# Twelve-row small products, values first, 128x128 filter tiles, shared filter copies and POOL in the block inversion

## What is computed

```
q = silu(dwconv(hs @ Wq, conv_q))        # causal convolutions with 4 taps over the tokens
k = silu(dwconv(hs @ Wk, conv_k))
v = silu(dwconv(hs @ Wv, conv_v))
beta = sigmoid(hs @ Wb)                  # one per head, 4 heads
q, k = l2norm(q), l2norm(k)              # per head: needs sums of squares over 64 channels
attn = where(strict, -(kb @ k.T), 0)     # in chunks of 32 tokens, kb = k * beta
T = inv(eye(32) - attn)                  # one unit triangular 32x32 inverse per chunk and head
fir = dwconv(v, 3 taps), dwconv(v, 15 taps), dwconv(v, 64 taps)   # per channel
```

## Time and profile before

| | |
|---|---|
| runs of the kernel | 1622.45, 1614.07, 1622.11 us; median 1622.11 |
| profiled execution | 1622.37 us, its span 1620.6 us |
| mean granted PE clock | 0.888 of full speed |
| PE busy | 1453.7 us (90%) |
| DVE, ACT, POOL busy | 878.0 (54%), 673.9 (42%), 527.5 (33%) us |
| the block in question | about 13 to 371 us of the span |

### The profile page before, as it was taken

How to read it: one execution, slowest core, us unless ns; L and a number is a source line. 1 busy time by engine, 2 the same in 40 slices (tenths; PEclk the granted TensorE clock), 3 DMA queues, 4 the chain that set the end, 5 groups by cost and what they waited for, 6 DMA issues and landing times. The chain is left out here.

```text
span 1620.6 us, 25691 instructions
## 1 busy us (share of the span) xinstructions
PE 1453.7 (90%) x8444; PEld 1138.4 (70%) x8445; DVE 878.0 (54%) x1708; ACT 673.9 (42%) x1269; POOL 527.5 (33%) x460
## 2 busy tenths in 40 slices
PE   4999976996999999939999999997979999999995
PEld 1666676985888888728888888884656666666643
DVE  4576636964999999934443444435622212212186
ACT  3333325995777777722333333331112222222214
POOL 3445510001455555523221222110314444444311
PEclk9778755557999999959999999977989999999998
DMA  3795365544333333213222201114011111111164
GB/s 86 158 223 151 102 193 146 139 154 118 98 92 91 91 95 92 59 54 107 69 95 95 77 30 60 43 40 146 14 52 55 56 57 55 57 57 55 49 201 136
DMA packets 149371, 151.89 MB, mean 94 GB/s; under 512 B 63952, under 2 KB 115760, under 8 KB 147760
## 3 DMA queue, kind: packets, MB, share of 16 engines
q1 hardware_dynamic: 136368, 117.34, 24.7%
q0 software_dynamic: 8320, 29.37, 7.0%
q10 hardware_dynamic: 4608, 4.20, 0.7%
HBM read 98.43 MB, written 42.99 MB: 87 GB/s over the span
## 5 line engine op out<-in xcount | busy, mean ns | idle before, releaser
L2405 DVE TENSOR_TENSOR hidden<-unit_psum,gate 128x352 f32<-128x352 f32 x72 | 37.8, 525 | 210.2 <-ACT gate L2368 210.2
L1818 POOL TENSOR_TENSOR scores<-scores,score_max 128x1024 f32<-128x1024 f32 x32 | 60.7, 1896 | 247.9 <-DVE score_max L1746 247.9
L498 PE MATMUL proj_psum<-window,toep 96*96 96x128 f32 x512 | 116.7, 401 | 22.0 <-DMA toep<-in_fir 11.5
L498 PEld LDWEIGHTS proj_psum<-window,toep 96*96 96x96 f32 x512 | 111.6, 256 | 26.9 <-DMA toep<-in_fir 15.6
L431 PE MATMUL proj_psum<-filtered 128*128 128x512 f32 x192 | 106.1, 705 | 24.4 <-DMA filtered<-in_xT 22.0
L569 ACT ACTIVATE filtered<-proj_psum 32x512 f32 (+1 forms) x192 | 112.7, 587 | 36.6 <-PE proj_psum L498 32.1
L618 DVE SCALAR_TENSOR_TENSOR filtered<-proj_psum,conv_taps,filtered 128x508 f32<-128x508 f32 (+1 forms) x144 | 95.5, 734 | 56.3 <-ACT filtered L523 56.3
L2336 PE MATMUL unit_psum<-wd,hiddenT 128*128 (+1 forms) x432 | 111.9, 395 | 13.7 <-issue 12.6
L2267 POOL DMA_INDIRECT unit_rows<-x_rows,token_of_slot x72 | 69.9, 970 | 127.1 <-PE unit_psum L2310 104.6
L2274 POOL DMA_INDIRECT outs<-unit_out,choice_of_slot x72 | 71.1, 987 | 99.3 <-DVE unit_out L2410 96.7
L2336 PEld LDWEIGHTS unit_psum<-wd,hiddenT 128*128 128x128 f32 (+1 forms) x432 | 76.4, 190 | 36.5 <-issue 28.8
(11 more groups left out here) (283 smaller groups left out, 3305.6 us busy)
## 6 DMA issues: line engine op xcount, KB each, us to landing
neg_decay_blocks<-in_gw1s POOLq DMA_DIRECT2D x8, 1280.0 KB, 9.7
ndg<-filtered SPq DMA_DIRECT2D x8, 1024.0 KB, 4.6
neg_decay_gram<-ndg SPq DMA_DIRECT2D x16, 512.0 KB, 3.8
ctxT_tiles<-in_ctxT SPq DMA_DIRECT2D x16, 512.0 KB, 3.6
gathered<-outs SPq DMA_DIRECT2D x32, 256.0 KB, 3.0
toep<-in_fir SPq DMA_DIRECT2D x64, 96.0 KB, 2.1
window<-value SPq DMA_DIRECT2D x32, 192.0 KB, 2.9
filtered<-in_xT SPq DMA_DIRECT2D x8, 512.0 KB, 4.3
```

Of the source, the lines that this page charges most:

```text
L498: mm = pe.matmul(fir_psum[0:NFIR * QUART, u, TC * w + c, :], toep[:, w, :, :, c].rearrange("p f t -> p (f t)"), window[:, u, :, :, TC * w ...
L1818: pool.tensor_tensor(sc[:, i % 2, t, :, :], sc[:, i % 2, t, :, :], wide(mx[:, t, :], [128, XH, L], 2), ALU.subtract).then_inc(shifted[t], 1)
```

## The change

- **Small products.** `small_rows` puts a 12-column selector (`small_weights`, 128 x 12) in the array and streams 512 columns of squares past it, 4 products, and 2 more with `Wb` over x. The result is 12 rows by 512 tokens. ACT copies it to SBUF (`keep_rows`), and `small_turn` turns it with four transposes. The copy of `Wb` into the selector is made by DVE before PE starts.
- **Order.** Values are projected first (2, 0, 1), the products of `small` come one block later around `projections(1)`, and each engine's order is rewritten to go with it. SP issues the chunk 2 windows and the rest of the tiles ahead of its waits for the last block's stores. The loops over chunks are written out.
- **Filters.** `toep` is laid out by channel, 128 x 128 for each, the rows from 96 and the columns from 96 being zero, and `window` has 128 rows. A half's transfer is one instead of two, with 4 KB a row of 96 rows.
- **Copies.** In chunks 0 to 4 and 15, DVE takes 4 of 12 pieces (even chunks) or 8 of 12 (odd ones).
- **Inversion.** POOL makes the product of group 1; DVE keeps the product of group 0 and both sums. DVE comes to the inversion after its copies of chunks 0 to 4.

```diff
+            def small_rows(n):
+                u = n % 2
+                pe.wait_ge(squared[0], n + 1)
+                pe.wait_ge(squared[1], n + 1)
+
+                pe.wait_ge(tanh_done, n)
+                pe.wait_ge(ssq_kept, n)
+                for t in range(2 * KD):
+                    pe.matmul(psum[0:3 * H, S_BANK, :], small_w[:, t, :], squares[:, u, t, :], start=(t == 0), stop=False)
+                for k in range(KD):
+                    mm = pe.matmul(psum[0:3 * H, S_BANK, :], small_w[:, 2 * KD + k, :], xT[:, u, k, :], start=False, stop=(k == KD - 1))
+                mm.then_inc(rows_mm, 1)
+
+            def small_turn(n):
+                pe.wait_ge(rows_kept, n + 1)
                 for q in range(BB):
-                    tok = slice(q * L, q * L + L)
-                    for t in range(2 * KD):
-                        pe.matmul(psum[:, S_BANK, 12 * q + 2 * t:12 * q + 2 * t + 2], squares[:, u, t, tok],
-                                  headsel[:, :], start=True, stop=True)
-                    for k in range(KD):
-                        mm = pe.matmul(psum[:, S_BANK, 12 * q + 8:12 * q + 12], xT[:, u, k, tok], wb[:, k, :],
-                                       start=(k == 0), stop=(k == KD - 1))
+                    mm = pe.transpose(psum[:, S_BANK, 3 * H * q:3 * H * q + 3 * H], small[0:3 * H, q * L:q * L + L],
+                                      M.ident[0:3 * H, 0:3 * H])
...
-                        mm = pe.matmul(fir_psum[0:NFIR * QUART, u, TC * w + c, :], toep[:, w, :, :, c].rearrange("p f t -> p (f t)"),
+                        mm = pe.matmul(fir_psum[:, u, TC * w + c, :], toep[:, w, c, :],
                                        window[:, u, :, :, TC * w + c].rearrange("p q b -> p (q b)"), start=True, stop=True)
                     mm.then_inc(half_done[w], 1)
 
+            for n in range(NBLK):
+                projections(2)(n)
+                if n >= 1:
+                    turn_values(1)(n - 1)
+                projections(0)(n)
+                if n >= 2:
+                    grams(0)(n - 2)
+                if n >= 1:
+                    small_rows(n - 1)
+                projections(1)(n)
+                if n >= 1:
+                    small_turn(n - 1)
+                if n >= 2:
+                    grams(1)(n - 2)
+                turn_values(0)(n)
+            last = NBLK - 1
+            turn_values(1)(last)
+            grams(0)(last - 1)
+            grams(1)(last - 1)
+            small_rows(last)
+            small_turn(last)
...
+        SHARED_CHUNKS = {0, 1, 2, 3, 4, NFC - 1}
+
+        def pieces(n, by_dve):
+
+            first = (2 - n % 2) if n in SHARED_CHUNKS else NFIR
+            return [(q, f) for f in (range(first, NFIR) if by_dve else range(first)) for q in range(NQ)]
...
+            for n in range(NBLK):
+                if n >= 2:
+                    decays(n - 2)
+                convolutions(2)(n)
+                if n >= 2:
+                    scale_grams(0)(n - 2)
+                convolutions(0)(n)
+                if n >= 1:
+                    keep_squares(n - 1)
+                if n >= 2:
+                    scale_grams(1)(n - 2)
+                convolutions(1)(n)
+            last = NBLK - 1
+            decays(last - 1)
+            scale_grams(0)(last - 1)
+            scale_grams(1)(last - 1)
+            keep_squares(last)
+            keep_pieces(0)
+            decays(last)
+            scale_grams(0)(last)
+            scale_grams(1)(last)
+            for n in range(1, 5):
+                keep_pieces(n)
 
             dve.wait_ge(nd_in, 32)
-
             for i in range(1, CB):
-                for g in range(2):
-                    blocks = slice(2 * g, 2 * g + 2)
-
-                    if i > 1:
-                        dve.wait_ge(inv_row[g], i - 1)
-                    p = prod[:, g, :, 0:i * i].rearrange("p c (k j) -> p c k j", j=i)
-                    dve.tensor_tensor(p, inv[:, blocks, 0:i, 0:i], wide(nd[:, blocks, i, 0:i], [128, 2, i, i], 2),
-                                      ALU.mult).then_inc(inv_mul[g], 1)
+                if i > 1:
+                    dve.wait_ge(inv_row[0], i - 1)
+                p = prod[:, 0, :, 0:i * i].rearrange("p c (k j) -> p c k j", j=i)
+                dve.tensor_tensor(p, inv[:, 0:2, 0:i, 0:i], wide(nd[:, 0:2, i, 0:i], [128, 2, i, i], 2),
+                                  ALU.mult).then_inc(inv_mul[0], 1)
                 for g in range(2):
                     blocks = slice(2 * g, 2 * g + 2)
                     dve.wait_ge(inv_mul[g], i)
                     p = prod[:, g, :, 0:i * i].rearrange("p c (k j) -> p c k j", j=i)
                     dve.tensor_reduce(inv[:, blocks, 0:i, i], p, AX.X, ALU.add).then_inc(inv_row[g], 1)
+
+            for n in range(5, NFC):
+                keep_pieces(n)
...
+            for i in range(1, CB):
+                if i > 1:
+                    pool.wait_ge(inv_row[1], i - 1)
+                p = prod[:, 1, :, 0:i * i].rearrange("p c (k j) -> p c k j", j=i)
+                pool.tensor_tensor(p, inv[:, 2:4, 0:i, 0:i], wide(nd[:, 2:4, i, 0:i], [128, 2, i, i], 2),
+                                   ALU.mult).then_inc(inv_mul[1], 1)
...
+            load_window(0)
+            load_window(1)
+            store_qk(last)
+            store_decays(last - 1)
+            load_toep(1)
+            load_window(2)
...
             sp.dma_start(nd[0:held, :, :, :], blocks[0:held]).then_inc(nd_in, 16)
-            store_decays(NBLK - 1)
+            store_decays(last)
+            load_toep(2)
+            load_window(3)
```

More of the change, by code:

```diff
@@ L371, in load_window @@
                     last = QUART * (q + 1)
-                    sp.dma_start(window[REACH - (last - first):REACH, u, q, :, :].rearrange("p b c -> p (b c)"),
-                                 M.value[first:last, chunk, :, :].rearrange("p k b c -> p (k b c)")).then_inc(window_in[u], 16)
+                    sp.dma_start(window[REACH - (last - first):REACH, n % 2, q, :, :].rearrange("p b c -> p (b c)"),
+                                 M.value[first:last, n, :, :].rearrange("p b c -> p (b c)")).then_inc(window_in[n % 2], 16)
             for i, w in enumerate((M.wq_dram, M.wk_dram, M.wv_dram)):
@@ L406, in _ @@
             sp.dma_start(nd[held:128, :, :, :], blocks[held:128]).then_inc(nd_in, 16)
[L408 to L411, removed]
+            for n in range(3, NFC):
+                load_toep(n)
+                if n + 1 < NFC:
+                    load_window(n + 1)
             for g in range(2):
@@ L435, in projections @@
                 return step
-            def small(n):
+            def small_rows(n):
                 u = n % 2
@@ L509, in _ @@
                 pe.wait_ge(gram_scaled[g], NBLK)
-            filters(0, 1)
-            with pe.Fori(1, NFC // 2) as j:
-                filters(j, 0)
-                filters(j, 1)
+            for n in range(1, NFC):
+                filters(n)
         @block.scalar
@@ L542, in silus, with keep_rows @@
                 return step
+            def keep_rows(n):
+                act.wait_ge(rows_mm, n + 1)
+                act.wait_ge(small_mm, n)
+                act.activation(small[0:3 * H, :], psum[0:3 * H, S_BANK, :], ACT.Copy).then_inc(rows_kept, 1)
             def tanhs(n):
@@ L589, in _ @@
-            with act.Fori(2, NFC // 2) as j:
-                keep(j, 0)
-                keep(j, 1)
+            for n in range(NBLK + 2):
+                if n >= 2:
+                    keep_rows(n - 2)
+                    tanhs(n - 2)
+                if 1 <= n <= NBLK:
+                    scaled_taps(1)(n - 1)
+                    silus(0)(n - 1)
+                    keep_values(0)(n - 1)
+                if n < NBLK:
+                    scaled_taps(2)(n)
+                if 1 <= n <= NBLK:
+                    silus(1)(n - 1)
+                if n < NBLK:
+                    scaled_taps(0)(n)
+                if 1 <= n <= NBLK:
+                    keep_values(1)(n - 1)
+                if n < NBLK:
+                    silus(2)(n)
@@ L593, in _ @@
+            for n in range(NFC):
+                wait_for_readers(act, n)
+                for w in range(2):
+                    act.wait_ge(half_done[w], n + 1)
+                for q, f in pieces(n, False):
+                    out, kept = piece(n, q, f)
+                    act.activation(out, kept, ACT.Copy).then_inc(kept_act[n % 2], 1)
         @block.vector
         def _(dve):
-            dve.memset(headsel[:, :], 0.0).then_inc(taps_step, 1)
+            dve.memset(small_w[:, :, :], 0.0).then_inc(taps_step, 1)
```

180 lines of the change are left out of this document (93 added, 87 removed).

## The result

The changed kernel is slower: 1640.73 us (median of 4 runs, 1638.22 to 1641.84) against 1618.09 of the kernel before (4 runs beside it); the ratio is 1.0137, 95% interval 1.0099 to 1.0176. The forecast was 1607, in a range of 1588 to 1631. The profiled span is 1638.5 us against 1620.6, and the first transfer of the next stage goes out at 391.9 us, where it went at 371.3: this block lost 20.6 us and the rest of the kernel gained 2.7. The mean granted clock rose all the same, from 0.888 to 0.934.

The account below looks back on a forecast made before the run. Bound: the block's end at 371.3 us, through PE at clock 0.80, DVE's inversion and the last filters. Projection -28, copies and later chunk 1 +25, inversion 0, end -12.6: 1622.4 minus 15.3 makes 1607, range 1588 to 1631.

Parts of the forecast that it names:

- The projection: Stage up to the first filter: 20.5 us a block instead of 23.9, first filter at 200 us, 28 earlier.
- The 20.5 us a block: Projection: PE work of 20.1 us a block at full clock plus 0.4 us for waits.
- The clock in the projection: Projection: full clock for the new order, 12-row products included; 3.60 us for 8 instructions.
- The rival that the 12 rows count as idle: Projection: 12-row products drop the clock to half, 25.2 us a block, 1640 us in all; chance 0.07.
- The filters' pace: Filter matmuls: pace does not follow the clock, 0.21 to 0.23 us each, a chunk of 32 stays at 7.3 us.
- DVE's copies: Filter copies out of PSUM on DVE: 0.74 us each, bounds 0.45 and 1; made before the inversion.
- From first filter to inversion: Stretch between first filter and inversion: starts at 200, inversion begins at 252.7 us; gives back 25 us.
- The inversion: Inversion on DVE and POOL: their products exclude each other, 95 us as before, no gain.
- the upper of my two bounds: POOL's inversion product: 2.2 ns an element, at most 46 us for the set, against 1.67 ns and 40 us.
- free overlap: Inversion: POOL's and DVE's products do not exclude each other, 78 us, 1590 us in all; chance 0.10.
- POOL first: Inversion: POOL's product takes the port before DVE's, 118 to 124 us, 1630 to 1636 in all; chance 0.13.
- The end: Behind the inversion: 8 us to the next stage instead of 20.6, block end at 356; worth 12.6 us.

Follow-up runs that it names:

- e1: The changed kernel with both squares of a block ahead of its gate transfers and gate sums in POOL's order; 1613.61 us, ratio 0.997 to the kernel before.
- e3: The changed kernel with all filter copies on ACT again, none on DVE; 1622.52 us, ratio 1.0027 to the kernel before.
- e8_before_gate_last: The kernel before with only POOL's order changed: gate transfers behind squares and power, sums one block later; 1634.7 us, ratio 1.0093.

## Why the prediction was wrong

- **The step that failed** is the one in "The projection" that reads: "POOL 5.4 for the power and some 4 for two squares. So neither is the bound". I counted what POOL computes for a block and left out what else its list holds between the squares: seven transfers of 1280 KB, none of which may be issued before the one ahead has landed, some 10 us after its own issue, and 9.8 us of gate sums. In the kernel before PE idled only 0.7 us ahead of its small products, and both squares of a block stood together; the change put one transfer of each of the first three blocks between the squares of q and of k. Price: 23.1 us of waits at four places, and 11.8 us more for the 12-row products of line 484 (41.3 us against 29.5 in e1), 10.6 of it right behind these waits, where the clock was at its half level for a part of them. With the list reordered the first filter came at 201.8 (200 forecast), and the time was 1613.6. The 20.5 us a block held for four of the seven pitches of e1 (19.3 to 20.8) and roughly for one (21.7); two were 24.2 and 23.4.
- **The clock in the projection** was right. The 12-row products with 512 columns streamed ran at 1.00 and took 3.60 us for 8; a clean block is 20.46. The rival that the 12 rows count as idle is false: the clock was at 0.50 behind the four pauses of 3.0 to 9.1 us, and at 1.00 in the sets that had none ahead.
- **The filters' pace** was right and is now shown: 0.226 us an instruction at full clock, and within 3% of it at half, against 0.119 at full clock without the step. The rule that I quoted in the prediction (the Trainium skill, SBUF — State Buffer, Door 1: The DMA port swizzle, on fp32 reads with a step over four elements) agrees with the two numbers at full clock, which lay the loss on the streamed side; at half clock this case shows no loss, 0.22 without the step.
- **DVE's copies** were right: 0.686 us each (0.74 forecast). From first filter to inversion took 52.9 us (52.7 forecast). That they give back most of the gain is what e3 shows.
- **The inversion** was right: 98.4 us, and 98.5 in e1 (95 forecast). DVE came first in each late row, POOL's product was drawn out by the length of DVE's, and the rest of it, 2.2 ns an element, is the upper of my two bounds. Neither free overlap nor POOL first.
- **The end** was right: 8.3 us behind the inversion (8).

So every term but one held within 4 us. That one was off by 32 us (first filter at 232.3 instead of 200), and 30.1 of it came back with the order of one queue.

## What to carry to other kernels

Before a ring of engines is made tighter, list all that each engine's queue holds within one turn, with its waits, also what belongs to another job and was free: a background transfer that waits for its predecessor costs nothing where that wait ends before the next urgent instruction could start, and up to the whole wait where it doesn't, as the pairs in `e8_before_gate_last` show. When helpers are moved to the engine with the last long serial job, what counts is the moment at which that job starts, not the engine's share of busy time. And a higher granted clock is no gain where the operand's step sets the pace, nor is the step's removal where the clock does: here only both together gave 1.9 times the pace.

## What the hardware did that I had not expected

- A POOL transfer that adds into SBUF, 1280 KB, takes 9.5 us to land (median of 7), so a chain of eight, each waited for in place, would fill some 76 us of a queue; that is an estimate, eight times 9.5.
- The same filter products ran at a granted clock of 1.00 with 128 rows and at 0.50 with 96, at nearly the same busy share (19.3 and 19.2 of 20 us), with 128 columns of the tile in both.
- Read without its step, the window gave 0.119 us an instruction at full clock and 0.22 at half; read with it, 0.226 and 0.23.
- One of DVE's smallest instructions, the `tensor_scalar` of 16 elements (line 705), took 2.85 us in the mean of the changed kernel, and 0.17 where POOL did nothing beside it. Its long instances lie beside POOL's squares and sums of gate rows, and a square beside it took 2.29 instead of 1.89. No run took this apart.
